# The expert layer of a graph and mixture-of-experts block: 35 pairs of blocks written out instead of 36, and a loop behind them that starts with an odd pair

## The chip, the cores and the metric

The kernel runs on one core of one Trainium2 chip. The metric is the time of one execution on the device, in microseconds (us), as the median of several runs. The engines are called PE (TensorE), DVE (VectorE), ACT (ScalarE), POOL (GpSimd) and SP (SyncE). All times below come from the three runs of the kernel before, or from one execution that the profiler recorded.

## What is computed

The input is 1250 nodes of width 512 and 40000 edges. A first part normalises the nodes, runs an attention over the edges and a linear attention beside it, and adds both. The part that matters here is the expert layer behind it:

```python
h = _ln(x, ln1_g, ln1_b).reshape(T, D)          # T = 1250, D = 512
logits = (h @ Wr) @ codebook.T / TEMP            # 64 experts
vals, idx = jax.lax.top_k(softmax(logits), 2)    # two experts a node, weights w
eh = silu(h @ W1[e] + b1[e])                     # 512 -> 256, for each expert e
eo = eh @ W2[e] + b2[e]                          # 256 -> 512
moe = sum of w * eo over the node's two experts
shared = (silu(h @ Ws1 + bs1) @ Ws2 + bs2) * 0.25   # 512 -> 1024 -> 512, every node
f = silu(_ln(moe + shared) @ Wf1 + bf1) @ Wf2 + bf2
return x + moe + shared + f
```

The 1250 nodes make 2500 assignments to 64 experts. With the reference's own inputs an expert gets from 7 to 88 of them: 59 experts have at most 64, five have more (71, 73, 79, 84 and 88).

## The kernel before

**Blocks and pairs.** The rows of an expert are cut into blocks of `R` = 64. Every expert has at least one block, so the inputs above fill 64 + 5 = 69 blocks. Blocks are numbered through, expert by expert, and two neighbouring blocks make a pair, which fills the 128 partitions. The number of blocks is only known on the chip. The kernel therefore has `PAIRS0` = 36 pairs (72 blocks) written out for every engine, and behind them a loop over two pairs at a time, which runs where there are more blocks. The bound of the loop, `H`, is worked out by DVE into `last`: (max(blocks, 69) - 1) >> 2, and every engine loads it. With `H` = 17 the loop is skipped and 2H + 2 = 36 pairs are done. A block without rows is worked on like any other; its lists of rows hold a number out of bounds, which the indirect DMAs leave out.

**One step of the expert loop.** Step p of PE has five parts, in this order:

- `hidden(p)` (L1739): the 512 to 256 product of pair p, with the weights `W1` of its two blocks,
- `result(p - 1)` (L1757): the 256 to 512 product of the pair before, with `W2`,
- the parts of `BESIDE[p]`: the shared network, cut into half products `("hidden", i, half)` (L1646) and thirds of a row tile `("shared", t, third)` (L1657, L1660), and a bias product (L1720); `parts_beside()` spreads these 50 parts over the `PAIRS0` steps in equal shares of columns,
- `hidden_transposes(p)` (L1747),
- `transposes(p + 2)` (L1729): the gathered rows `Zg` of the pair after next.

**Who feeds it.** POOL's queue has, for each p, the gather of pair p + 2 (L603) once `transposes(p)` is done, then the scatter of pair p - 1 (L608) once ACT has copied its result from PSUM (`eo`, L1347). So the gather that `transposes(p + 3)` needs at the end of step p + 1 stands behind the scatter of pair p - 1, and that behind `result(p - 1)` in step p. In steps 2 to 11 an addition on POOL (L624) stands between scatter and gather. SP loads the weights: for pair p, the two `W1` of 0.5 MB (L482) once `hidden(p - 2)` is done and the two `W2` (L485) once `result(p - 2)` is done. Buffers `Zg`, `hgT`, `eh`, `ehT` and `eo` are double, by the parity of the pair, and the weights lie in four places, two for each parity.

**The tail.** After the last result PE does the shared rows of tiles 8 and 9 (L1657, L1660), then the last network (L1802, L1810, L1818). POOL sends the last scatter, SP waits for both parities' scatters (`y_out[0]`, `y_out[1]`) and reads all of `y_d` back as `Yt` (L512). DVE weighs and adds the two results of each node (L1138), sums up the statistics, and works out the scale factors (L1147, L1149) from ACT's square roots (L1382); ACT normalises into `fz` (L1389), which PE transposes (L1802).

Of the kernel before, what the change touches and what calls it, by code (L numbers as in the profile page):

```python
# [6 lines left out]
F32 = mybir.dt.float32  # L7
# [25 lines left out]
PAIRS0 = 36  # L33
NP = 52
# [140 lines left out]
def block_kernel(nc, A, out):  # L175
    ctx = ExitStack()
    with ctx:
# [44 lines left out]
        carry = keep("carry", [1, 4, 1], F32)  # L222
# [183 lines left out]
        y_out = [sem(f"y_out{u}") for u in range(2)]  # L406
        yt_in = [sem(f"yt_in{i}") for i in range(YB)]
# [16 lines left out]
        def _(sp):  # L424
# [50 lines left out]
            def owners(g):  # L475
                return nc.values_load_multi_w_load_instructions(
                    owner[0:1, 4 * g:4 * g + 4] if isinstance(g, int) else owner[0:1, bass.ds(4 * g, 4)],
                    engines=[mybir.EngineType.SP], min_val=0, max_val=E - 1,
                    skip_runtime_bounds_check_because="an expert's number, held to E - 1 as it is made")[1]
# [7 lines left out]
            def group_weights(h):  # L487

                e = owners(h + 1)
                for u in range(2):  # L490
                    at_least(sp, h_done, 2 * h + u + 1)
                    first_weights(e[2 * u], 2 * u)
                    first_weights(e[2 * u + 1], 2 * u + 1)
                    at_least(sp, e_done, 2 * h + u + 1)
                    second_weights(e[2 * u], 2 * u)
                    second_weights(e[2 * u + 1], 2 * u + 1)

            for h in range(-1, PAIRS0 // 2 - 1):
                group_weights(h)
            H = sp.value_load(last[0:1, 0:1], min_val=PAIRS0 // 2 - 1, max_val=NP // 2 - 1)  # L500
# [22 lines left out]
        def _(gp):  # L523
# [68 lines left out]
            gp.drain().then_inc(idxg_made, PAIRS0 - 2)  # L592
            gp.drain().then_inc(idxs_made, PAIRS0 - 2)
# [31 lines left out]
            H = gp.value_load(last[0:1, 0:1], min_val=PAIRS0 // 2 - 1, max_val=NP // 2 - 1)  # L625
            with gp.If(H > PAIRS0 // 2 - 1):
                with gp.Fori(PAIRS0 // 2 - 1, H) as h:
                    for u in range(2):
                        wait_alone(tr_done, 2 * h + u + 3, 0)
                        nc.gpsimd.tensor_copy(idxg[:, u, :], gat[:, bass.ds(2 * h + u + 4, 1)]).then_inc(idxg_made, 1)  # L630
                        wait_alone(idxg_made, 2 * h + u + 1, 1)
                        gather(u, idxg[:, u, :])
                        wait_alone(e_read, 2 * h + u + 2, 2)
                        nc.gpsimd.tensor_copy(idxs[:, 1 - u, :], lst[:, bass.ds(2 * h + u + 1, 1)]).then_inc(idxs_made, 1)
                        wait_alone(idxs_made, 2 * h + u + 1, 3)
                        scatter(1 - u, idxs[:, 1 - u, :])
# [8 lines left out]
            for u in range(2):  # L645
                wait_alone(zg_in[u], 16 * H + 32, 0)
# [4 lines left out]
        def _(v):  # L651
# [377 lines left out]
            for k, M in ((0, M1), (1, M2)):  # L1029
# [4 lines left out]
                if k == 0:  # L1034
# [6 lines left out]
                    V_.tensor_scalar(last_i[:, :], counted[:, 0:1], -1.0, None, ALU.add)  # L1041
# [78 lines left out]
            H = v.value_load(last[0:1, 0:1], min_val=PAIRS0 // 2 - 1, max_val=NP // 2 - 1)  # L1120
            with v.If(H > PAIRS0 // 2 - 1):
                with v.Fori(PAIRS0 // 2 - 1, H) as h:
                    for u in range(2):
# [746 lines left out]
```

## Time and profile before

| | |
|---|---|
| three runs, median (lowest to highest) | 888.22 us (887.15 to 889.78) |
| the profiled execution's own time | 888.11 us |
| its span | 886.1 us, 11946 instructions |
| granted TensorE clock, mean | 0.996 of full speed |
| moved by DMA | 129.81 MB, mean 146 GB/s |

The span is the time from the first to the last instruction that the profiler saw. The execution's own time is 2.0 us longer, the start and end around the span. Rows of the timeline merge instructions of one line that follow each other; a matmul's length is modelled and reaches into the next row, so the time that a piece takes on PE is the difference between two starts. The expert loop's steps stand between about 546 and 817 us, the tail behind them.

### The profile page before, as it was taken

The numbers are of one execution on the slowest core, as the hardware profiler recorded it, in microseconds if no ns is written. First come the engines' busy times: TensorE is split into PE (matmuls) and PEld (weight loads), VectorE is DVE, ScalarE is ACT, GpSimd is POOL, SyncE is SP. The second block draws the span as 40 slices with busy tenths as digits, with TensorE's granted clock in tenths as the row PEclk, the third lists the DMA queues.
The fourth block names the chain that finished last, engine by engine and source line by source line (L and its number), as shares of the span: only waits on it lengthen the run. The fifth ranks groups of instructions, "written<-read, shape, count | busy, mean of one in ns | idle before, by whom it ended". The sixth has DMA issues, their size and how long they took to land.

```text
span 886.1 us, 11946 instructions
## 1 busy us (share of the span) xinstructions
PE 844.7 (95%) x3978; PEld 492.3 (56%) x3978; DVE 517.3 (58%) x1317; ACT 287.5 (32%) x560; POOL 153.1 (17%) x168
## 2 busy tenths in 40 slices
PE   3999999999989999999999999999999999999897
PEld 2565556655567444444456587456456545654464
DVE  7787677666776999999855584222223222222472
ACT  4531111200105666666334332223122212222283
POOL 6100002300100000000000211344422222222340
PEclk9999999999999999999999999999999999999999
DMA  9410000000327350510211524898898888895723
GB/s 274 166 49 1 1 1 1 1 0 1 136 96 173 84 117 1 116 49 1 68 62 46 181 106 163 276 314 317 302 320 318 321 315 289 320 317 209 201 54 94
DMA packets 41340, 129.81 MB, mean 146 GB/s; under 512 B 8393, under 2 KB 8835, under 8 KB 40639
## 3 DMA queue, kind: packets, MB, share of 16 engines
q1 hardware_dynamic: 32955, 110.76, 39.0%
q0 software_dynamic: 7872, 17.94, 5.6%
q8 instruction: 33, 0.54, 0.3%
q10 hardware_dynamic: 452, 0.34, 0.2%
q14 instruction: 28, 0.23, 0.1%
HBM read 118.48 MB, written 19.68 MB: 156 GB/s over the span
## 4 chain that ended last, share of the span: by engine, by line
PE 69%; DVE 12%; DMA 6%; issue 5%; DVEq 4%; ACT 2%; SPq 1%; POOL 1%; POOLq 0%; ACTq 0%
PE ps L1480 8%; DVE att L934 7%; PE ps L1739 7%; PE ps L1660 6%; PE ps L1757 6%; PE ps L1646 6%; DMA Zg<-z_d,gat 4%; PE ps L1458 4%; PE ps L1524 4%; PE ps L1611 4%; PE ps L1532 4%; PE ps L1441 3%; PE ps L1602 2%; PE ps L1575 2%; PE ps L1729 2%
## 5 line engine op out<-in xcount | busy, mean ns | idle before, releaser
L1085 DVE TENSOR_SCALAR hgT<-ps,cols 128x128 f32<-128x128 f32 x152 | 51.8, 403 | 152.1 <-PE ps L1729 142.1
L934 DVE TENSOR_TENSOR att<-es,C 125x832 f32<-125x832 f32 (+1 forms) x120 | 116.2, 1010 | 4.7 <-ACT es L1262 4.0
L1262 ACT ACTIVATE es<-ps 125x832 f32<-125x832 f32 (+1 forms) x120 | 95.4, 867 | 54.7 <-PE ps L1564 53.9
L1575 PE MATMUL ps<-att,V 125*64 125x416 f32 (+1 forms) x480 | 96.7, 525 | 5.5 <-DVE att L934 4.5
L1660 PE MATMUL ps<-Ws_s,hsT 128*125 128x512 f32 x160 | 75.0, 607 | 0.0
L1646 PE MATMUL ps<-hT,Ws_s 128*128 128x250 f32 x320 | 72.8, 379 | 0.4 <-issue 0.4
L1480 PE MATMUL ps<-mW,xnT 128*125 128x512 f32 x160 | 72.2, 594 | 0.0
L1739 PE MATMUL ps<-W,hgT 128*64 128x256 f32 x576 | 70.1, 385 | 0.4 <-DVE hgT L1085 0.4
L1646 PEld LDWEIGHTS ps<-hT,Ws_s 128*128 128x128 f32 x320 | 58.9, 189 | 19.4 <-issue 13.2
L1757 PE MATMUL ps<-W,ehT 128*64 128x512 f32 x288 | 68.0, 592 | 0.7 <-ACT ehT L1339 0.7
L608 POOL DMA_INDIRECT y_d<-eo,lst x35 | 35.6, 1018 | 177.2 <-ACT eo L1347 177.2
L753 DVE TENSOR_SCALAR ohB<-iotaW,key 125x200 bf16<-125x200 f16 x320 | 64.6, 265 | 0.0
L1575 PEld LDWEIGHTS ps<-att,V 125*64 125x64 f32 x480 | 29.1, 136 | 56.1 <-issue 31.5
L1564 PE MATMUL ps<-Qst,Kst 128*125 128x416 f32 (+1 forms) x240 | 56.9, 370 | 1.8 <-DVE C L895 0.7
L1347 ACT COPY eo<-ps 128x512 f32<-128x512 f32 x36 | 21.1, 585 | 114.7 <-PE ps L1757 114.7
L1339 ACT ACTIVATE ehT<-ps,b1T 128x64 f32<-128x64 f32 x144 | 33.4, 317 | 74.5 <-PE ps L1747 71.1
L1564 PEld LDWEIGHTS ps<-Qst,Kst 128*125 128x125 f32 x240 | 41.2, 185 | 28.8 <-ACT es L1262 18.4
L1660 PEld LDWEIGHTS ps<-Ws_s,hsT 128*125 128x125 f32 x160 | 28.1, 187 | 46.0 <-issue 46.0
L1739 PEld LDWEIGHTS ps<-W,hgT 128*64 128x64 f32 x576 | 38.1, 136 | 20.4 <-DVE hgT L1085 0.5
L566 POOL DMA_DIRECT2D z_d<-yz x10 | 5.4, 536 | 239.2 <-DVE yz L969 239.2
L1441 PEld LDWEIGHTS ps<-ohB,ohA 125*128 125x128 bf16 x320 | 30.8, 114 | 28.2 <-issue 25.5
L757 DVE TENSOR_TENSOR Cx<-Cx,ps 128x200 f32 x80 | 28.5, 356 | 29.9 <-PE ps L1441 17.2
(249 smaller groups left out, 1204.1 us busy)
## 6 DMA issues: line engine op xcount, KB each, us to landing
W<-in_W SPq DMA_DIRECT2D x144, 512.0 KB
Kst<-qk_d SPq DMA_DIRECT2D x32, 156.2 KB, 5.6
Qst<-qk_d SPq DMA_DIRECT2D x32, 156.2 KB, 5.8
Yt<-y_d SPq DMA_DIRECT2D x10, 448.0 KB
Ws_s<-in_Ws SPq DMA_DIRECT2D x2, 2048.0 KB, 9.9
qk_d<-qk_hi POOLq DMA_DIRECT2D x4, 625.0 KB, 3.6
qk_d<-qk_lo POOLq DMA_DIRECT2D x4, 625.0 KB, 4.7
z_d<-yz POOLq DMA_DIRECT2D x10, 250.0 KB, 2.7
```

The lines of the kernel that those rows point to most:

```text
L753: i = V_.tensor_scalar(ohB[:, s, j, :], iotaW[:, :], key[:, bass.ds(k + j, 1)], None, ALU.is_equal)
L934: V_.tensor_tensor(att[:, n % AB, :, 0:w], es[:, n % EB, :, 0:w], C[:, s, o:o + w].unsqueeze(1).to_broadcast([P, 2, w]), ALU.mult).then_in ...
L1085: i = V_.tensor_scalar(hgT[:, u, k, :], bank(u, 128, 128, k * 128), col("g1", k), col("b1ln", k), ALU.mult, ALU.add)
L1262: S_.activation(es[:, n % EB, :, 0:w], scores_of(n, w), ACT.Exp, scale=float(DK) ** -0.5).then_inc(s_exp, 1)
L1441: i = MM(bank(b, WN), ohA[:, s, :, j], ohB[:, s, j, :], start=j == 0, stop=j == EG - 1)
L1480: i = MM(bank(b, D, P), xnT[:, k, t * P:t * P + P], mW[:, 1 + w, k, :], start=k == 0, stop=k == KD - 1)
L1564: k = MM(scores_of(n, w)[:, j, :], Kst[:, h % 4, s * P:s * P + P], Qst[:, h % 4, o:o + w], start=True, stop=True)
L1575: k = MM(sums_of(i, 64 * j, 64, w), V[:, s, pair, j:j + 2, :], att[:, n % AB, j, 0:w], start=s == 0, stop=s == T - 1, skip_group_check=True)
L1646: j = MM(bank(b, 250, 128, 250 * half), Ws1_s[:, k, (2 * g + half) * 128:(2 * g + half + 1) * 128], hT[:, k, c * 250:c * 250 + 250], start ...
L1660: i = MM(bank(b, D, P), hsT[:, t // 2 % 2, k, (t % 2) * P:(t % 2) * P + P], Ws2_s[:, k, :], start=False, stop=k == DSH // 128 - 1)
L1739: i = MM(bank(2, DFF, 128, DFF * u)[R * j:R * j + R], hgT[:, u, k, R * j:R * j + R], W1[2 * u + j][:, k, :], start=k == 0, stop=k == KD - ...
L1757: i = MM(bank(4 + u, D)[R * j:R * j + R], ehT[:, u, m, R * j:R * j + R], W2[2 * u + j][:, m, :], start=m == 0, stop=m == 1, skip_group_che ...
```

## The change

`PAIRS0` becomes 35. The written-out part then ends with an even pair (34, buffers of parity 0), where it ended with an odd one (35, parity 1). The loop behind it still does two pairs an iteration, now first the odd and then the even one, and its bound becomes (max(blocks, 67) - 3) >> 2, with 2H + 3 pairs done. With 69 blocks H is 16, the lower bound, the loop is skipped, and 35 pairs (70 blocks) are done. The closing scatter is that of parity 0. SP's wait at the end for both parities is replaced: POOL waits for `y_out[1]` after it has sent the last scatter, does an addition of one element and raises `odd_written`; SP waits for `odd_written` and then for `y_out[0]`. The queue of SP is written per pair instead of per two pairs, in the same order. `parts_beside()` is unchanged but spreads over 35 steps.

```diff
-PAIRS0 = 36
+PAIRS0 = 35
...
-        carry = keep("carry", [1, 4, 1], F32)
+        carry = keep("carry", [1, 5, 1], F32)
...
+            def pair_weights(p, u, e):
+
+                at_least(sp, h_done, p - 1)
+                first_weights(e[0], 2 * u)
+                first_weights(e[1], 2 * u + 1)
+                at_least(sp, e_done, p - 1)
+                second_weights(e[0], 2 * u)
+                second_weights(e[1], 2 * u + 1)
+
+            for p in range(0, PAIRS0, 2):
+                e = owners(2 * p)
+                pair_weights(p, 0, e[0:2])
+                if p + 1 < PAIRS0:
+                    pair_weights(p + 1, 1, e[2:4])
+            H = sp.value_load(last[0:1, 0:1], min_val=PAIRS0 // 2 - 1, max_val=NP // 2 - 2)
...
-            for u in range(2):
-                sp.wait_ge(y_out[u], 16 * H + 16)
+            sp.wait_ge(odd_written, 1)
+            sp.wait_ge(y_out[0], 16 * H + 32)
...
-            gp.drain().then_inc(idxg_made, PAIRS0 - 2)
-            gp.drain().then_inc(idxs_made, PAIRS0 - 2)
+            gp.drain().then_inc(idxg_made, PAIRS0 - 1)
+            gp.drain().then_inc(idxs_made, PAIRS0 - 1)
...
-            wait_alone(y_out[1], 16 * H, 2)
-            nc.gpsimd.tensor_copy(idxs[:, 1, :], lst[:, bass.ds(2 * H + 1, 1)]).then_inc(idxs_made, 1)
-            wait_alone(idxs_made, 2 * H + 1, 3)
-            wait_alone(e_read, 2 * H + 2, 1)
-            scatter(1, idxs[:, 1, :])
+            wait_alone(y_out[0], 16 * H + 16, 2)
+            nc.gpsimd.tensor_copy(idxs[:, 0, :], lst[:, bass.ds(2 * H + 2, 1)]).then_inc(idxs_made, 1)
+            wait_alone(idxs_made, 2 * H + 3, 3)
+            wait_alone(e_read, 2 * H + 3, 1)
+            scatter(0, idxs[:, 0, :])
+            wait_alone(y_out[1], 16 * H + 16, 4).then_inc(odd_written, 1)
...
-                    V_.tensor_scalar(last_i[:, :], counted[:, 0:1], -1.0, None, ALU.add)
+                    V_.tensor_scalar(last_i[:, :], counted[:, 0:1], -3.0, None, ALU.add)
...
             with pe.If(H > PAIRS0 // 2 - 1):
                 with pe.Fori(PAIRS0 // 2 - 1, H) as h:
...
                     hidden(2 * h + 3, h + 1, 1)
                     result(2 * h + 2, h + 1, 0)
                     hidden_transposes(2 * h + 3, 1)
                     transposes(2 * h + 5, h + 2, 1)
-            result(2 * H + 1, H, 1)
+                    hidden(2 * h + 4, h + 2, 0)
+                    result(2 * h + 3, h + 1, 1)
+                    hidden_transposes(2 * h + 4, 0)
+                    transposes(2 * h + 6, h + 3, 0)
+            result(2 * H + 2, H + 1, 0)
...
-            pe.wait_ge(tr_read, 2 * H + 4)
-            pe.wait_ge(h_read, 2 * H + 2)
-            pe.wait_ge(x_read, 2 * H + 2)
-            pe.wait_ge(e_read, 2 * H + 2)
+            pe.wait_ge(tr_read, 2 * H + 5)
+            pe.wait_ge(h_read, 2 * H + 3)
+            pe.wait_ge(x_read, 2 * H + 3)
+            pe.wait_ge(e_read, 2 * H + 3)
```

The other hunks change the bounds of `value_load` and the order of the pairs in the loops of POOL, DVE and ACT in the same way. Lines from about L407 on stand 1 to 6 lines lower in the changed kernel.

**Where the instructions move.** The spreading over 35 steps moves parts between neighbouring steps. On PE the ends of steps 5, 6 and 7 read before (L1646 is a half product of the shared network as x4, two as x8, L1747 and L1729 close a step, and the rows left out are the pair's own products):

```order
L1646 MATMUL ps<-hT,Ws_s 128x250 x8
L1747 MATMUL ps<-ident,eh 128x128 x2
L1729 MATMUL ps<-ident,Zg 128x128 x4
...
L1646 MATMUL ps<-hT,Ws_s 128x250 x4
L1747 MATMUL ps<-ident,eh 128x128 x2
L1729 MATMUL ps<-ident,Zg 128x128 x4
...
L1646 MATMUL ps<-hT,Ws_s 128x250 x8
L1747 MATMUL ps<-ident,eh 128x128 x2
L1729 MATMUL ps<-ident,Zg 128x128 x4
```

and in the changed kernel, where the same three lines are L1652, L1753 and L1735:

```order
L1652 MATMUL ps<-hT,Ws_s 128x250 x8
L1753 MATMUL ps<-ident,eh 128x128 x2
L1735 MATMUL ps<-ident,Zg 128x128 x4
...
L1652 MATMUL ps<-hT,Ws_s 128x250 x8
L1753 MATMUL ps<-ident,eh 128x128 x2
L1735 MATMUL ps<-ident,Zg 128x128 x4
...
L1652 MATMUL ps<-hT,Ws_s 128x250 x4
L1753 MATMUL ps<-ident,eh 128x128 x2
L1735 MATMUL ps<-ident,Zg 128x128 x4
```

The two steps with one and two half products have changed places: the step with only one is now step 7, behind two full ones.

POOL's queue, from the end of the loop to the first addition of the tail, reads before (the last rows of the loop are left out; L600 is the one-element addition that a wait stands before, L638 the copy of the list of rows, L608 the scatter, L644 the addition of the tail):

```order
L599 REGISTER_ALU
L600 TENSOR_TENSOR carry<-eps 1x1
L638 ISA
L638 COPY idxs<-lst 128x1
L600 TENSOR_TENSOR carry<-eps 1x1
L599 REGISTER_ALU
L600 TENSOR_TENSOR carry<-eps 1x1
L608 DMA y_d<-eo,idxs 2500x512
L644 TENSOR_TENSOR XR<-XR,HM 125x512 x10
```

and in the changed kernel:

```order
L604 ISA
L605 TENSOR_TENSOR carry<-eps 1x1
L643 ISA
L643 COPY idxs<-lst 128x1
L604 REGISTER_ALU
L605 TENSOR_TENSOR carry<-eps 1x1 x2
L613 DMA y_d<-eo,idxs 2500x512
L605 TENSOR_TENSOR carry<-eps 1x1
L650 TENSOR_TENSOR XR<-XR,HM 125x512 x10
```

One addition of one element, the one that raises `odd_written`, now stands between the last scatter and the ten additions of the tail.

## Rows read from the trace of the kernel before

**Rows 1.** The page, part 1: busy microseconds, share of the span, instructions
```profile
PE 844.7 (95%) x3978; PEld 492.3 (56%) x3978; DVE 517.3 (58%) x1317; ACT 287.5 (32%) x560; POOL 153.1 (17%) x168
```

**Rows 2.** Stretches: length, busy PE, PEld, DVE, ACT, POOL, clock, DMA share, GB/s
```profile
546.00:812.00 266.00, 262.01 (x1396) 148.69 (x1394) 69.01 (x188) 61.39 (x198) 82.75 (x79) 1.00 0.87 306
```

**Rows 3.** What PE waited for, 540 to 836 us: total, times, longest
```profile
PE ps L1729 <- DMA Zg<-z_d,gat: 4.0, 6, 1.0
```

**Rows 4.** Timeline of PE: start, length, [idle before]; one step, one half product
```profile
593.60 1.96 PE L1646 MATMUL ps<-hT,Ws_s 128*128 128x250 f32 x8
595.39 0.39 PE L1747 MATMUL ps<-ident,eh 128*128 128x128 f32 x2
...
802.76 1.95 PE L1739 MATMUL ps<-W,hgT 128*64 128x256 f32 x16
804.53 1.89 PE L1757 MATMUL ps<-W,ehT 128*64 128x512 f32 x8
806.35 2.84 PE L1660 MATMUL ps<-Ws_s,hsT 128*125 128x512 f32 x6
809.03 0.39 PE L1747 MATMUL ps<-ident,eh 128*128 128x128 f32 x2
809.26 0.65 PE L1729 MATMUL ps<-ident,Zg 128*128 128x128 f32 x4
809.83 1.95 PE L1739 MATMUL ps<-W,hgT 128*64 128x256 f32 x16
```

**Rows 5.** Timeline of PE: two of the six stalls in the expert loop
```profile
658.21 0.75 PE L1729 MATMUL ps<-ident,Zg 128*128 128x128 f32 x4 [0.97 <-DMA Zg<-z_d,gat]
...
757.33 0.75 PE L1729 MATMUL ps<-ident,Zg 128*128 128x128 f32 x4 [0.48 <-DMA Zg<-z_d,gat]
```

**Rows 6.** Timeline of POOL: the gathers that these two waited for, and a later one
```profile
649.92 1.03 POOL L603 DMA_INDIRECT Zg<-z_d,gat  x1 [0.30 <-issue]
...
749.61 1.03 POOL L603 DMA_INDIRECT Zg<-z_d,gat  x1 [0.30 <-issue]
...
809.18 1.03 POOL L603 DMA_INDIRECT Zg<-z_d,gat  x1 [0.30 <-issue]
```

**Rows 7.** Tail, timelines of PE, ACT and DVE: shared rows to scale factors
```profile
817.70 1.94 PE L1757 MATMUL ps<-W,ehT 128*64 128x512 f32 x8 [0.73 <-ACT ehT L1339]
...
835.70 0.63 PE L1802 MATMUL ps<-ident,fz 125*128 125x125 f32 x4
...
836.84 0.30 ACT L1382 ACTIVATE rs<-mv,eps 125x1 f32<-125x1 f32 x1
...
828.33 1.59 DVE L1138 SCALAR_TENSOR_TENSOR HM<-Yt,wtop,HM 125x512 f32<-125x512 f32 x2 [9.95 <-DMA Yt<-y_d]
...
837.17 0.16 DVE L1147 RECIPROCAL rs<-rs 125x1 f32<-125x1 f32 x1 [1.07 <-ACT rs L1382]
```

**Rows 8.** Tail, timelines of POOL and SP: the last scatter, the first read-back
```profile
814.93 1.01 POOL L608 DMA_INDIRECT y_d<-eo,lst  x1 [4.72 <-ACT eo L1347]
...
821.17 1.02 POOL L608 DMA_INDIRECT y_d<-eo,idxs  x1 [0.56 <-issue]
...
823.93 10.37 SPq L512 DMA_DIRECT2D Yt<-y_d  x20
```

**Rows 9.** Half-microsecond stretches after the last two scatters, columns as rows 2
```profile
816.50:817.00 0.50, 0.48 (x4) 0.28 (x3) 0.50 (x1) 0.47 (x3) 0.04 (x1) 1.00 0.31 99
...
822.50:823.00 0.50, 0.50 (x3) 0.26 (x2) 0.00 (x0) 0.00 (x0) 0.00 (x0) 1.00 0.08 1
```

**Rows 10.** DMA by queue, 814 to 830 us: packets, MB, share
```profile
q0 software_dynamic: 160, 0.05, 1.2%
```

**Rows 11.** The page, part 6: a plain write to HBM from POOL, us to landing
```profile
z_d<-yz POOLq DMA_DIRECT2D x10, 250.0 KB, 2.7
```

**Rows 12.** Timelines of POOL and PE: a gather on idle DMA engines
```profile
540.12 1.03 POOL L603 DMA_INDIRECT Zg<-z_d,gat  x1 [0.30 <-issue]
...
543.52 0.75 PE L1729 MATMUL ps<-ident,Zg 128*128 128x128 f32 x4 [0.36 <-DMA Zg<-z_d,gat]
```

More of the change, by code:

```diff
@@ L406, in block_kernel @@
         y_out = [sem(f"y_out{u}") for u in range(2)]
+        odd_written = sem("odd_written")
         yt_in = [sem(f"yt_in{i}") for i in range(YB)]
@@ L485, in second_weights @@
                 sp.dma_start(W2[s][:, :, :], A["W2"][bass.ds(e, 1)].rearrange("e (p m) n -> p (e m) n", m=2)).then_inc(w2_in[s], 16)
-            def group_weights(h):
-                e = owners(h + 1)
-                for u in range(2):
[L491 to L500, printed above, removed]
+            def pair_weights(p, u, e):
[11 more added lines that the diff above has]
+            H = sp.value_load(last[0:1, 0:1], min_val=PAIRS0 // 2 - 1, max_val=NP // 2 - 2)
             with sp.If(H > PAIRS0 // 2 - 1):
                 with sp.Fori(PAIRS0 // 2 - 1, H) as h:
-                    group_weights(h)
-            for u in range(2):
-                sp.wait_ge(y_out[u], 16 * H + 16)
+                    e = owners(4 * h + 6)
+                    pair_weights(2 * h + 3, 1, e[0:2])
+                    pair_weights(2 * h + 4, 0, e[2:4])
+            sp.wait_ge(odd_written, 1)
+            sp.wait_ge(y_out[0], 16 * H + 32)
             y_v = y_d.rearrange("(t p k) d -> t p k d", p=P, k=TOPK)
@@ L1119, in _ @@
                 rows_turned(p + 2, p % 2)
-            H = v.value_load(last[0:1, 0:1], min_val=PAIRS0 // 2 - 1, max_val=NP // 2 - 1)
+            H = v.value_load(last[0:1, 0:1], min_val=PAIRS0 // 2 - 1, max_val=NP // 2 - 2)
             with v.If(H > PAIRS0 // 2 - 1):
                 with v.Fori(PAIRS0 // 2 - 1, H) as h:
-                    for u in range(2):
-                        hidden_kept(2 * h + u + 2, u)
-                        rows_turned(2 * h + u + 4, u)
+                    for i in range(2):
+                        hidden_kept(2 * h + i + 3, 1 - i)
+                        rows_turned(2 * h + i + 5, 1 - i)
             def output(t):
@@ L1775, in _ @@
                 transposes(p + 2, p // 2 + 1, p % 2)
-            H = pe.value_load(last[0:1, 0:1], min_val=PAIRS0 // 2 - 1, max_val=NP // 2 - 1)
+            H = pe.value_load(last[0:1, 0:1], min_val=PAIRS0 // 2 - 1, max_val=NP // 2 - 2)
             with pe.If(H > PAIRS0 // 2 - 1):
                 with pe.Fori(PAIRS0 // 2 - 1, H) as h:
-                    hidden(2 * h + 2, h + 1, 0)
-                    result(2 * h + 1, h, 1)
-                    hidden_transposes(2 * h + 2, 0)
-                    transposes(2 * h + 4, h + 2, 0)
                     hidden(2 * h + 3, h + 1, 1)
```

36 lines of the change are left out of this document (18 added, 18 removed).

## The prediction

> **What bounds the kernel now.** I read the page's busy line first: PE is busy for 844.7 us of a span of 886.1, DVE for 517.3, ACT for 287.5, POOL for 153.1 [rows 1]. A step taken off PE's queue is therefore a step off the span, unless PE waits in that stretch for somebody else. The stretch of the expert loop, 546 to 812 us, says how much it does: PE is busy for 262.01 of 266.00 us, at a granted clock of 1.00 of full speed, 2.4 GHz. The DMA engines are close behind, with a share of 0.87 at 306 GB/s [rows 2]. The waits of PE name the whole difference: 4.0 us in six waits, the longest 1.0, all of them for the gather of `Zg` [rows 3]. So PE sets the pace of the loop, and transfers take 4.0 us of it. In the tail PE, ACT and DVE hand work to each other; that is looked at below.
>
> **Does the change do what it says?** The pair that goes must be one without rows. The counts in the section on what is computed give 64 + 5 = 69 blocks, so 35 pairs hold them all with one block spare. The trace agrees. After the scatter of pair 34, issued at 814.93 [rows 8], 0.5 us at 99 GB/s moved 50 KB, which is 24 rows of 2 KB; after that of pair 35, issued at 821.17, the stretch in which its data would move shows 1 GB/s [rows 9]. All that the software queue moved from 814 to 830 us is 0.05 MB [rows 10]. Pair 35 is empty, H becomes (69 - 3) >> 2 = 16, and the loop behind is skipped as now.
>
> **The change part by part.**
>
> *The pair's own work on PE.* By differences of starts [rows 4]: hidden 804.53 - 802.76 = 1.77, result 806.35 - 804.53 = 1.82, the two hidden transposes 809.26 - 809.03 = 0.23, the four row transposes 809.83 - 809.26 = 0.57. Together 4.39 us, with nothing beside it: PE has no gap between these rows. The shared parts stay, in number and length; they only sit in 35 steps. The end of the loop keeps its form too: the last step before it and the last result do the same work on the other parity. Term: **-4.4 us**.
>
> *The pair's work elsewhere.* Four weight loads of 0.5 MB, a gather, a scatter without rows, four scalings on DVE and one copy, one copy and four activations on ACT. None of these engines is behind which PE waited in the loop [rows 3]. Term: 0. If that cover were gone it could only be a gain, since all of it is work removed.
>
> *The waits for the gathers.* A gather is sent after the result of step p, and needed at the end of step p + 1. The result before the late gather ended at 806.35, the gather was issued at 809.18, 2.83 us later [rows 4, 6]. From there to its transposes PE has the shared parts b(p), 0.23 + 0.57 + 1.77 + 1.82 + 0.23 = 4.62 us of pair work, and b(p + 1). So the gather has b(p) + b(p + 1) + 1.8 us. A third of a shared row tile is 809.03 - 806.35 = 2.68 us, a half product 595.39 - 593.60 = 1.79 [rows 4]; two thirds in a row give 7.2 us, one half product beside two give 1.79 + 3.58 + 1.8 = 7.2 too. Measured from issue to the stalled transposes, gathers took 658.21 - 649.92 = 8.29 and 757.33 - 749.61 = 7.72 us [rows 5, 6], and the stalls of 0.97 and 0.48 are what is over, to 0.2 us. Short neighbours make stalls, but not always, since a stall or a long step lets the transfers catch up. I went through both tables of parts and counted the neighbours with b(p) + b(p + 1) up to 5.6 us, from step 1 on, without the last three, behind which the weights run out: 18 before and 15 after. In six places something was late before. Some move: the one at the end of step 6 goes to step 7 (the order rows above), where the single half product now stands. The same share of 15 gives 4.0 x 15 / 18 = 3.3 us, a gain of 0.7; nothing but the backlog decides where, so 0 is as near. I take the middle, **-0.3 us**. The bounds: -4.0 if all six vanish, and +2.0 if two of the neighbours that got by now stall by the longest wait of 1.0 each.
>
> *The tail.* It starts from the last result, so all of it moves forward with it. Two things are new there. First, the last scatter now carries the 24 rows of pair 34, where it was empty. The empty one took 823.93 - 821.17 = 2.76 us from issue to SP's first read-back [rows 8]; a plain write of 250 KB from POOL lands after 2.7 us [rows 11], a gather of up to 128 rows on idle engines is used 543.52 - 540.12 = 3.40 us after its issue [rows 12]. So the rows cost from -0.1 to +0.6 us; I take 0.2, nearer the write. Second, the read-back has some slack: DVE, after its first tiles, waits 1.07 us at 837.17 for ACT's square root of 836.84, and ACT is late because it copies what PE transposed at 835.70, when the shared rows were done [rows 7]. A read-back up to 1.07 us later changes nothing. Term: **0**; without that cover, +0.2.
>
> *The new handshake.* POOL's extra wait is for a scatter sent one step earlier, 6.2 us before [rows 8], and queued behind it on POOL are only the additions of the tail, which wait for DVE. `odd_written` rises about one issue (1.02 us) after the last scatter starts, while that one needs 2.76 to land. SP has nothing else to do. Term: 0.
>
> By the Trainium skill, page "DMA: Bandwidth & Descriptors", section "Anatomy of one DMA", a DMA has a fixed cost of about 2 us, most of it the receipt of the write, and the receipt is slowest when the target is HBM. If an empty scatter had no receipt to wait for, the real one would cost up to 2 us more, an estimate from that page, and 0.9 of it would be beyond the slack. The trace speaks against: the empty scatter's 2.76 us already are a full write's 2.7.
>
> **Sum.** 888.11 - 4.4 - 0.3 = 883.4 us for the profiled execution. It stands 0.1 under the median of the three runs, 888.22, so I predict **883.5 us**.
>
> **The rivals.**
>
> *Transfers pace the loop.* For it: a share of 0.87 and 306 GB/s. A pair's weights are 4 x 0.5 MB = 2.1 MB, at 306 GB/s 6.9 us, which would be saved instead of 4.4: 881.3 us. At the extreme all waits go: 883.5 + 0.3 - 4.0 = 879.8. Against: PE lost only 4.0 us in all, and the pair removed is the last one, behind which nothing else is loaded. Chance 0.07.
>
> *The gain is partly given back.* The new grouping stalls more, up to +2.0, or the last scatter with its rows is beyond the slack, 3.4 - 2.76 would not be enough, so it would have to land like a gather in the loaded loop: 8.29 - 2.76 - 1.07 = +4.5 at the very most, in a tail where no weights are moving. With one of them in part, 884.7 to 886.5 us. The rule on the write receipt belongs here: a scatter that moves rows lands later than an empty one, here by 1.07 + 0.9 us at most if it is to cost the 0.9, and that gives 883.5 + 0.9 = 884.4; chance of it 0.06, inside the forecast's own range. The rest of this rival has 0.12.
>
> *The loop is entered.* If more than 70 blocks were counted, 35 pairs would be followed by an iteration of two. This is the one that ends slower. Its steps have no shared parts to hide behind: transfers then set the pace, at least the 6.9 us of weights a pair, at most the 2.83 + 8.29 us from a result to the next rows. That is 883.5 + 2 x 6.9 = 897 to 883.5 + 2 x 11.1 = 906 us. It decides from block 71 on. Against: 69 blocks, and no rows moved in pair 35 [rows 9, 10]. Chance 0.02.
>
> **The numbers.** About 0.3%, 2.7 us, is what a measurement of this kernel can tell from no change, so faster means under 885.5. The forecast, 882.3 to 884.7, has 0.78 with the receipt in it, transfers that pace 0.07, given back 0.12, the loop 0.02, and 0.01 is left for what I do not see. Faster: 0.78 + 0.07 + half of 0.12 = 0.91, of which I take one point off for the spread of the runs, 887.15 to 889.78: 0.90. Within 0.3%: 0.07. Slower: 0.03. The range that leaves out no more than 2 in 10 reaches half way into the two neighbours: 881.7 to 885.3.
>
> **What would show it.** In the profile after: 35 copies to `eo`, 140 weight loads, 37 gathers, and PE busy for about 840.3 us. The start of the first product of the loop is the same as now, and the last result starts 4 to 5 us before 817.70. PE's waits for `Zg` sum to 2.5 to 4.5 us, with one at step 7 rather than at step 6. SP's read-back starts 2.7 to 3.4 us after the last scatter, and DVE's wait for ACT's square root shrinks from 1.07 by what the scatter gained; if that wait is gone the tail's term was wrong. If PE's waits changed by more than 1 us, the term of the gathers was. Copies into `idxg` on POOL, or more than 35 pairs, would make all of it wrong.

## The result and the profile after

| | before | changed |
|---|---|---|
| median of 9 runs | 887.92 us (885.59 to 890.45) | 883.93 us (881.92 to 885.45) |
| ratio, 95% interval | | 0.9949 [0.9936, 0.9961] |
| profiled execution, time and span | 888.11 and 886.1 us | 884.23 and 882.5 us |
| first `hidden` starts | 544.62 us | 546.57 us |
| loop: from there to the last `result` | 273.08 us | 267.88 us |
| tail: from there to the end of the span | 68.40 us | 68.05 us |

The changed kernel is faster by 0.51%, 4.5 us (3.5 to 5.7), by the ratio; the two medians differ by 4.0 us. The two profiles differ by 3.6 us in span. That difference is made of three parts: 546.57 - 544.62 = +1.95 us ahead of the loop, -5.20 us in it, -0.35 us behind it. The lines of the page for the changed kernel (L1745 is `hidden`, L1763 `result`, L1735 the row transposes):

```profile
span 882.5 us, 11853 instructions
...
PE 841.4 (95%) x3948; PEld 490.4 (56%) x3948; DVE 515.1 (58%) x1312; ACT 286.3 (32%) x555; POOL 151.9 (17%) x167
...
W<-in_W SPq DMA_DIRECT2D x140, 512.0 KB, 6.7
```

The counts are those forecast: 140 loads of `W` for 144, 37 gathers and 35 copies to `eo`. PE is busy 3.3 us less than the 844.7 of [rows 1]. Its waits from 535 to 836 us, which answer to [rows 3] (total, times, longest):

```profile
PE ps L1735 <- DMA Zg<-z_d,gat: 2.7, 4, 1.0
...
PE ps L1745 <- DVE hgT L1091: 1.0, 1, 1.0
PE ps L1763 <- ACT ehT L1345: 0.9, 1, 0.9
```

The waits for `Zg` are 2.7 us in four places, for 4.0 us in six. PE's timeline, with the first product of the loop, the four stalls, and the last result:

```profile
546.57 1.95 PE L1745 MATMUL ps<-W,hgT 128*64 128x256 f32 x16 [0.98 <-DVE hgT L1091]
...
591.50 0.75 PE L1735 MATMUL ps<-ident,Zg 128*128 128x128 f32 x4 [0.50 <-DMA Zg<-z_d,gat]
...
697.89 0.75 PE L1735 MATMUL ps<-ident,Zg 128*128 128x128 f32 x4 [0.74 <-DMA Zg<-z_d,gat]
...
758.93 0.75 PE L1735 MATMUL ps<-ident,Zg 128*128 128x128 f32 x4 [0.46 <-DMA Zg<-z_d,gat]
...
791.35 0.75 PE L1735 MATMUL ps<-ident,Zg 128*128 128x128 f32 x4 [0.97 <-DMA Zg<-z_d,gat]
...
814.45 1.94 PE L1763 MATMUL ps<-W,ehT 128*64 128x512 f32 x8 [0.94 <-ACT ehT L1345]
```

The stalls stand at the ends of steps 5, 19, 27 and 31. The tail, in the timelines of POOL, SP, ACT and DVE, which answers to [rows 7, 8]:

```profile
817.91 1.03 POOL L613 DMA_INDIRECT y_d<-eo,idxs  x1 [0.57 <-issue]
818.97 0.18 POOL L605 TENSOR_TENSOR carry<-eps 1x1 f32<-1x1 f32 x1
...
820.25 10.31 SPq L517 DMA_DIRECT2D Yt<-y_d  x20
...
833.58 0.30 ACT L1388 ACTIVATE rs<-mv,eps 125x1 f32<-125x1 f32 x1
...
833.91 0.16 DVE L1153 RECIPROCAL rs<-rs 125x1 f32<-125x1 f32 x1 [1.56 <-ACT rs L1388]
```

The addition at 818.97 raises `odd_written`, long before SP's read-back at 820.25. From the last scatter to the read-back it takes 820.25 - 817.91 = 2.34 us, for 2.76 before, although this scatter carries rows. DVE then waits 1.56 us for ACT's square root, for 1.07 before: the read-back came earlier, and what ended the wait is still ACT, behind PE's shared rows.

Further on in the tail PE waits 2.18 us for `fz` in both kernels, and the product behind it does not take equally long. In the kernel before (L1810) and in the changed one (L1816):

```profile
839.92 5.21 PE L1810 MATMUL ps<-fT,Wf_s 128*128 128x250 f32 x16 [0.67 <-ACT fT L1367]
...
836.67 3.65 PE L1816 MATMUL ps<-fT,Wf_s 128*128 128x250 f32 x16 [0.67 <-ACT fT L1373]
```

To the next start it is 844.97 - 839.92 = 5.05 us before, where the granted clock fell to 0.64 between 841 and 844 us, and 840.20 - 836.67 = 3.53 us after, where it stayed at 1.00. The time did not change: the product with `f1T` that follows starts 6.55 us after these rows in both (846.47 and 843.22), since in the changed kernel PE waits 1.56 us for ACT there, for 0.39 before.

**The 1.95 us ahead of the loop are not the change's.** No instruction moves there. Stretches of the profile (length, busy PE, PEld, DVE, ACT, POOL, granted clock, DMA share, GB/s) of the changed kernel:

```profile
513.00:519.00 6.00, 5.73 (x72) 5.41 (x72) 3.72 (x14) 1.32 (x3) 0.76 (x1) 0.86 0.01 3
519.00:522.00 3.00, 3.00 (x9) 2.34 (x9) 2.78 (x6) 0.00 (x0) 0.00 (x0) 0.50 0.00 0
522.00:525.00 3.00, 3.00 (x11) 2.51 (x10) 2.44 (x9) 0.00 (x0) 0.00 (x0) 0.65 0.26 59
525.00:528.00 3.00, 3.00 (x16) 2.69 (x15) 2.92 (x3) 1.53 (x3) 0.00 (x0) 1.00 1.03 370
```

and of the kernel before:

```profile
513.00:519.00 6.00, 4.94 (x71) 4.25 (x69) 3.85 (x13) 1.53 (x3) 0.76 (x1) 1.00 0.01 3
519.00:522.00 3.00, 3.00 (x18) 2.68 (x17) 2.66 (x4) 0.00 (x0) 0.00 (x0) 1.00 0.00 0
```

In the changed kernel's profile the granted clock is 0.50 of full speed from 519 to 522 us, which is 1.2 GHz, and 0.65 in the three after. Before it fell PE did the many small products that count the experts' rows. The 64 matmuls of the shared network behind them show the cost. In the changed kernel they start at 519.26 and the next line at 535.24:

```profile
519.26 16.14 PE L1652 MATMUL ps<-hT,Ws_s 128*128 128x250 f32 x64
535.24 1.54 PE L1707 MATMUL ps<-slots,rowhot 125*128 125x156 bf16 x20
```

15.98 us. In the kernel before:

```profile
519.70 13.76 PE L1646 MATMUL ps<-hT,Ws_s 128*128 128x250 f32 x64
533.30 1.54 PE L1701 MATMUL ps<-slots,rowhot 125*128 125x156 bf16 x20
```

13.60 us, the same work: 2.38 us less, and the rest of the 1.95 is a start that was 0.44 us later before. I looked at the stretch from 505 to 528 us in all 14 profiles of this study: the clock was lowered somewhere in it in 10 of them, in kernels with 36 pairs and with 35, and not in 4; the kernel before is one of the 4 and the changed one of the 10. `table_alone` and `table_again` below are one and the same kernel, profiled twice, the first time without the lowering and the second time with it. In 9 of the 10 the clock fell behind the small products, and the 64 matmuls took 14.8 to 16.5 us for 13.6; in `plain_waits` it fell ahead of them, at 504 to 510 us. The first `hidden` starts at 543.2 to 545.0 us in the four and at 544.3 to 547.6 in the others. Over many executions the two kernels are alike in this: the mean granted clock is 0.9942 over the nine of the changed kernel, and 0.9945 over 27 of the kernel before that were timed beside `table_alone`.

### The profile page after: what moved, and what is told of

The parts are those of the page before. It is cut to its first block, busy times and chain, and to the rows that moved or that the text cites. A ratio compares the mean times of both kernels' runs of the same rounds, so it can differ in the third digit from the quotient of the medians.

```text
span 882.5 us, 11853 instructions
## 1 busy us (share of the span) xinstructions
PE 841.4 (95%) x3948; PEld 490.4 (56%) x3948; DVE 515.1 (58%) x1312; ACT 286.3 (32%) x555; POOL 151.9 (17%) x167
## 4 chain that ended last, share of the span: by engine, by line
PE 68%; DVE 12%; DMA 6%; issue 5%; DVEq 4%; ACT 2%; POOL 1%; SPq 1%; POOLq 0%; ACTq 0%
PE ps L1486 8%; DVE att L940 7%; PE ps L1666 6%; PE ps L1745 6%; PE ps L1652 6%; PE ps L1763 6%; DMA Zg<-z_d,gat 5%; PE ps L1464 4%; PE ps L1530 4%; PE ps L1617 4%; PE ps L1538 4%; PE ps L1447 3%; PE ps L1608 2%; PE ps L1581 2%; PE ps L1735 2%
## 5 line engine op out<-in xcount | busy, mean ns | idle before, releaser
L1652 PE MATMUL ps<-hT,Ws_s 128*128 128x250 f32 x320 | 74.7, 388 | 0.4 <-issue 0.4
L1652 PEld LDWEIGHTS ps<-hT,Ws_s 128*128 128x128 f32 x320 | 60.7, 194 | 18.9 <-issue 12.1
L1745 PE MATMUL ps<-W,hgT 128*64 128x256 f32 x560 | 68.2, 385 | 1.0 <-DVE hgT L1091 1.0
L1763 PE MATMUL ps<-W,ehT 128*64 128x512 f32 x280 | 66.1, 592 | 0.9 <-ACT ehT L1345 0.9
L1745 PEld LDWEIGHTS ps<-W,hgT 128*64 128x64 f32 x560 | 37.1, 136 | 20.4 <-DVE hgT L1091 1.2
```

The costliest lines, as they stand in the source:

```text
L1652: j = MM(bank(b, 250, 128, 250 * half), Ws1_s[:, k, (2 * g + half) * 128:(2 * g + half + 1) * 128], hT[:, k, c * 250:c * 250 + 250], start ...
L1745: i = MM(bank(2, DFF, 128, DFF * u)[R * j:R * j + R], hgT[:, u, k, R * j:R * j + R], W1[2 * u + j][:, k, :], start=k == 0, stop=k == KD - ...
L1763: i = MM(bank(4 + u, D)[R * j:R * j + R], ehT[:, u, m, R * j:R * j + R], W2[2 * u + j][:, m, :], start=m == 0, stop=m == 1, skip_group_che ...
```

## The experiments

The prediction left three things to be shown. My theory: the gain is the pair's 4.4 us of work on PE, which sets the pace; the waits for `Zg` move a little, and come from the gather's place in POOL's queue; transfers are not the bound. The rivals: the regrouping of the shared parts brings the time, or the pair is worth the 6.9 us of its transfers. In the table, the loop and the waits for `Zg` (those over 0.2 us, in the loop) are from each profile; the ratio is to the kernel before, timed on the same chip.

| kernel | pairs | ratio, 95% interval | loop, us | waits for Zg, at the ends of steps |
|---|---|---|---|---|
| before | 36 | 1 | 273.08 | 4.0: 4, 6, 14, 17, 23, 27 |
| changed | 35 | 0.9949 [0.9936, 0.9961] | 267.88 | 2.7: 5, 19, 27, 31 |
| table_alone | 36 | 1.0002 [0.9986, 1.0017] | 276.28 | 4.1: 11, 14, 19, 27, 31 |
| table_again | 36 | one execution | 271.89 | 2.4: 12, 19, 31, 34 |
| pair_alone | 35 | 0.9961 [0.9946, 0.9975] | 267.84 | 2.7: 4, 14, 17 |
| loads_kept | 35 | 0.9949 [0.9934, 0.9964] | 268.44 | 2.9: 2, 12, 19, 27, 31 |
| loads_removed | 36 | 0.9997 [0.9983, 1.0012] | 273.03 | 3.1: 2, 6, 9, 14, 23 |
| plain_waits | 35 | 0.9941 [0.9928, 0.9954] | 269.19 | 3.6: 2, 4, 8, 14, 19, 24, 31 |
| constants_36 | 36 | one execution | 273.14 | 2.4: 14, 24, 27, 29 |
| gather_first_36 | 36 | 0.9953 [0.9936, 0.9969] | 269.31 | none |
| gather_first | 35 | 0.9901 [0.9886, 0.9915] | 264.19 | none |
| first_weights_first | 35 | 0.9892 [0.9864, 0.9920] | 262.76 | none |
| loop_entered | 33 + 2 | 0.9945 [0.9924, 0.9966] | 268.41 | 3.3: 14, 22, 33 |
| loop_taken_37 | 35 + 2 | 1.0097 [1.0071, 1.0124] | 282.26 | 5.2: 2, 19, 31, 35 |

### The table alone, and the pair alone

```diff
 # table_alone, on the kernel before
-        table[min(PAIRS0 - 1, done * PAIRS0 // total)].append(part)
+        table[min(PAIRS0 - 2, done * (PAIRS0 - 1) // total)].append(part)
 # pair_alone, on the changed kernel
-        table[min(PAIRS0 - 1, done * PAIRS0 // total)].append(part)
+        table[min(PAIRS0 - 1, done * (PAIRS0 + 1) // total)].append(part)
```

> The kernel before with its 36 pairs, but with the shared parts spread over the first 35 steps as in the changed kernel, so that step 35 has only the pair's own work. Theory (the gain is the pair's own 4.4 us on PE, and the regrouping moves only the waits for gathers): between -1.3 and +0.3 us against before in the loop, plus what the bare step 35 exposes, since its hidden transposes, activation and result now follow each other with nothing beside them: about +1 us for the copy of the hidden rows. Together within 1 us of before, and PE's waits for Zg sum to 2.5 to 4.5 us. Rival (the regrouping is what brings the time): 2 us or more faster than before. Rival (transfers pace): no change.

> The changed kernel with 35 pairs, but with the shared parts spread as over 36 steps, the parts of step 35 joined to step 34. Theory: -4.4 us from the removed pair, and the stalls of before in steps 4 to 27 at their old places, so 3.4 to 4.6 us faster than before and within 1 us of the changed kernel; PE's waits for Zg sum to 3.5 to 4.5 us, with those of before at the ends of steps 4, 6, 14, 17, 23 and 27. Rival (the regrouping is a good part of the gain): only 2 to 3 us faster than before. Rival (transfers pace the loop): 6 us or more.

The table alone changed nothing (-0.1 to +0.2%). The pair alone gave 0.9961, 3.5 us of 888.5 (2.2 to 4.8), against 4.5 with both; the intervals overlap, so whether the table adds a microsecond can't be told. Its loop, 267.84 us, is that of the changed kernel to 0.04. The rival of the regrouping falls. Of my expectation for the places, three of six came true (4, 14, 17).

The first profile of `table_alone` had a loop of 276.28 us, 3.2 over the kernel before, which its times don't show. Step 20 was long. PE's timeline there:

```profile
698.26 0.75 PE L1729 MATMUL ps<-ident,Zg 128*128 128x128 f32 x4 [1.78 <-DMA Zg<-z_d,gat]
698.94 2.96 PE L1739 MATMUL ps<-W,hgT 128*64 128x256 f32 x16
701.68 2.62 PE L1757 MATMUL ps<-W,ehT 128*64 128x512 f32 x8
```

and the stretches around it (columns as above):

```profile
700.00:702.00 2.00, 2.00 (x12) 1.19 (x10) 0.48 (x3) 0.00 (x0) 0.00 (x0) 0.50 0.99 385
702.00:704.00 2.00, 2.00 (x8) 0.39 (x4) 0.37 (x1) 0.00 (x0) 0.00 (x0) 0.72 0.54 212
```

After a wait of 1.78 us the granted clock fell to 0.50, and `hidden` took 2.74 us and `result` 2.55 to the next start, for 1.77 and 1.82. So a stall can cost nearly its length again. The same kernel was profiled once more:

> The kernel before with 36 pairs and the shared parts spread over the first 35 steps, once more, for its profile: in the first one step 20 took 1.7 us longer than the same step of the changed kernel, with its products slower at an unchanged number. Theory (a granted clock that fell for one moment after a wait of 1.8 us): a chance event that does not return here; the loop from the first hidden product to the last result takes 273 to 275 us. Rival (the regrouping with 36 pairs is slower): 276 us again, with the same step long.

Its loop was 271.89 us, with no wait over 0.9 us and no long step: chance, as the theory said, and even below the 273 I had given. A wait of 1.55 us in `pair_alone` and one of 1.51 in `loop_entered` were followed by a clock of 1.00, so the length alone does not decide. The tail shows it better: the wait of 2.18 us for `fz` is there in all 14 profiles, and the clock fell behind it in 12, but not in the changed kernel and in `loads_kept`.

### The weight loads alone

```diff
 # loads_kept, on the changed kernel
+            pair_weights(PAIRS0, 1, e[2:4])
...
+            for j in (2, 3):
+                sp.wait_ge(w1_in[j], 16 * (PAIRS0 // 2 + 1))
+                sp.wait_ge(w2_in[j], 16 * (PAIRS0 // 2 + 1))
             sp.wait_ge(odd_written, 1)
 # loads_removed, on the kernel before
-                for u in range(2):
+                for u in range(1 if isinstance(h, int) and h == PAIRS0 // 2 - 2 else 2):
                     at_least(sp, h_done, 2 * h + u + 1)
```

In `loads_removed` PE's waits for the weights of pair 35 ask for one load less.

> The changed kernel, to which the four weight loads of a pair 35 are given back (2.1 MB that nobody reads, sent where the kernel before sends them), without its products, gather or scatter. Theory (PE paces the loop): within 0.5 us of the changed kernel, so 3.6 to 4.9 us faster than before. Rival (transfers pace, and a pair is worth its 6.9 us of weights): most of the gain is gone, within 1.5 us of before.

> The kernel before with its 36 pairs, but without the four weight loads of pair 35, whose products then read what lies in their places; pair 35 has no rows, so no output depends on it. Theory (PE paces the loop): within 0.5 us of before, and PE's waits for Zg unchanged to 1 us, since the loads fall in the last three steps. Rival (transfers pace): 2 us or more faster than before.

With the four loads given back the ratio is 0.9949, the changed kernel's own; with them taken away from the kernel before it is 0.9997. The last pair's 2.1 MB are worth nothing that shows in either; the intervals reach some 1.3 us to each side. The rival of the transfers falls for this pair, by both runs.

### Gathers ahead of scatters

```diff
             gather(1, gat[:, 1:2])
+            gp.wait_ge(tr_done, 1)
+            gather(0, gat[:, 2:3])
             for p in range(PAIRS0):
-                gp.wait_ge(tr_done, p + 1)
-                gather(p % 2, gat[:, p + 2:p + 3])
+                gp.wait_ge(tr_done, p + 2)
+                gather((p + 1) % 2, gat[:, p + 3:p + 4])
                 if p:
                     gp.wait_ge(e_read, p)
                     scatter((p - 1) % 2, lst[:, p - 1:p])
```

The loop behind has the same shift.

> The changed kernel with POOL's queue in another order: the gather of pair p + 3 is sent before the scatter of pair p - 1, once the transposes of pair p + 1 are done, and no longer behind the result of pair p - 1. It is then issued about 5 us earlier in its step. Theory (the waits for Zg come from the gather's place behind the scatter): PE's waits for Zg, 2.7 us in the changed kernel, fall under 0.3 us, and the time is 2 to 3.5 us below the changed kernel, near 881.3 us, 6.5 to 8 us below the kernel before. Rival (the DMA engines are full, and what is late then is the weights): PE waits for the transfers of W instead, and the time is within 1 us of the changed kernel.

> The kernel before, 36 pairs, with the same new order on POOL. Theory: its 4.0 us of waits for Zg go, 3 to 4.5 us faster than before, and the difference to the same edit with 35 pairs is the removed pair's own work alone, 4.4 us in the loop. Rival (the pair is worth its transfers, 6.9 us): that difference is 6 us or more.

881.18 us and 0.9901, 8.8 us below the kernel before, a little more than the 6.5 to 8 expected. On the same chip `plain_waits`, which does what the changed kernel does, had 883.90 and 0.9941, so the new order is worth 2.7 us by the medians and 3.6 by the ratios, and 267.88 - 264.19 = 3.7 in the loop of the profiles (5.0 against the profile of `plain_waits`, which had more waits). What PE waits for from 540 to 836 us (L1747 is `hidden`, L1765 `result`):

```profile
PE ps L1747 <- DMA W<-in_W: 1.1, 3, 0.7
PE ps L1747 <- DVE hgT L1093: 1.0, 1, 1.0
PE ps L1765 <- ACT ehT L1347: 0.8, 1, 0.8
```

No wait for `Zg` is left, as the theory said; 1.1 us of waits for `W` have come up, as the rival said, but they are less than what went. With 36 pairs the same edit gives 0.9953. The difference of the two is 0.52%, 4.6 us, the removed pair with the gathers' waits out of the way in both: the 4.4 us of PE's work, not 6.9, which lies just outside what the two intervals leave together, some 2.6 to 6.6 us. In the profiles the loops differ by 269.31 - 264.19 = 5.1 us, 0.6 of it waits for `W`, 1.7 us with 36 pairs and 1.1 with 35.

### First weights first

```diff
 # SP's order, on gather_first:   W1(p), W2(p), W1(p + 1), W2(p + 1), ...
 # becomes:                       W1(p + 1), W2(p), W1(p + 2), W2(p + 1), ...
+                first_of(p, e[0:2])
+                if old is not None:
+                    second_of(p - 1, old)
...
+                    first_of(p + 1, e[2:4])
+                    old = e[2:4]
+                second_of(p, e[0:2])
```

> The changed kernel with gathers ahead of scatters, and in SP's queue the W1 of pair p + 1 ahead of the W2 of pair p. In the profile with gathers ahead PE waited 1.1 us for transfers of W, each time at the first product of a step. Theory (W1 is needed 1.8 us before the W2 that stands ahead of it in the queue): those waits go and no wait for W2 comes up, 1 us or less faster than with gathers ahead alone, near 880.3 us. Rival (the transfers only change places, and W2 or the gathers are late by the same): no gain, or a loss of up to 1 us.

878.94 us, ratio 0.9892, 9.6 us below the kernel before. It is 0.8 us below `gather_first` by the ratios, with intervals that overlap, so the times do not show a gain of this step by itself; the profile does, 262.76 us of loop for 264.19. All that PE waits for from 540 to 836 us (L1762 is `hidden`, L1780 `result`, L1825 and L1833 are in the tail):

```profile
PE ps L1825 <- ACT fz L1412: 2.2, 1, 2.2
PE ps L1762 <- DVE hgT L1108: 1.0, 1, 1.0
PE ps L1780 <- ACT ehT L1362: 0.8, 1, 0.8
PE ps L1833 <- ACT fT L1390: 0.7, 1, 0.7
```

Not one wait for a transfer is listed. PE is busy for 261.92 of the loop's 262.76 us, and the one wait in it is that of 0.84 for its last product; the wait of 0.98 stands ahead of the first. This version beats both kernels.

### The loop, priced

```diff
 # loop_entered, on the changed kernel
-PAIRS0 = 35
+PAIRS0 = 33
 # loop_taken_37, on the changed kernel
-                    V_.tensor_scalar(counted[:, 0:1], base_s[0:1, E:E + 1], 1.0 / R, 2.0 * PAIRS0 - 3.0, ALU.mult, ALU.max)
+                    V_.tensor_scalar(counted[:, 0:1], base_s[0:1, E:E + 1], 1.0 / R, 2.0 * PAIRS0 + 1.0, ALU.mult, ALU.max)
```

> The changed kernel with 33 pairs written out, so that with 69 blocks the loop behind runs once and does pairs 33 and 34: again 35 pairs in all. The shared parts are spread over 33 steps. This measures what the loop would have cost. Theory (bare steps are paced by the gathers and weights): the two looped steps take 2 x 6.9 to 2 x 11.1 us where two written-out ones without their shared parts take 2 x 4.4, so 5 to 13 us slower than the changed kernel. Rival (the loop costs no more than its branches): within 2 us of it.

> The changed kernel with the lower bound of counted blocks raised from 67 to 71, so that its loop runs once although 69 blocks are filled, and 37 pairs are done, 35 and 36 without rows. This is the rival that ends slower, by itself. Its price as predicted: 13.8 to 22 us over the changed kernel, 897 to 906 us. Corrected theory, from the run with 33 pairs written out, whose two looped steps took 6.3 and 5.5 us and not 6.9 or more, because the weights that they wait for were loaded beside longer steps: 11 to 13 us over the changed kernel, 895 to 897 us. And if a scatter without rows takes longer than one with 24 rows, SP's first read-back is again 2.7 us or more after the last scatter, since pair 36 has no rows; if the parity or the handshake decided, 2.3 to 2.4 us.

With two of the 35 pairs in the loop, the ratio is 0.9945, no slower than with all written out. I had expected 5 to 13 us. The two looped steps on PE:

```profile
801.59 1.95 PE L1745 MATMUL ps<-W,hgT 128*64 128x256 f32 x16 [0.40 <-DMA W<-in_W]
803.34 1.92 PE L1763 MATMUL ps<-W,ehT 128*64 128x512 f32 x8
...
807.21 0.75 PE L1735 MATMUL ps<-ident,Zg 128*128 128x128 f32 x4 [1.51 <-DMA Zg<-z_d,idxg]
807.89 1.95 PE L1745 MATMUL ps<-W,hgT 128*64 128x256 f32 x16
...
813.40 1.94 PE L1763 MATMUL ps<-W,ehT 128*64 128x512 f32 x8 [0.58 <-ACT ehT L1345]
```

From 801.59 to 813.40 us, 11.8 us for both: 2 x 4.4 of work, waits of 1.51 and 0.58, the last of which the changed kernel has too (0.94), and 0.9 us in gaps too short to be listed; a wait of 0.40 stands ahead. So the bare steps cost 3 us more at most. The step that failed in my price is that a bare step is paced by the 6.9 us of its weights: PE waited 0.40 us for weights in these two. That they had been loaded beside the longer steps ahead is my reading. In the profile's loop 0.5 us of it is left, 268.41 for 267.88; waits for `Zg` ahead were shorter by 0.9 and the last wait by 0.4, and the remaining 1 us I did not follow up.

With two pairs more than the changed kernel, the loop costs 1.0097 - 0.9949 = 1.48%, 13.1 us (10 to 17 by the intervals), and 282.26 - 267.88 = 14.4 us in the profile. It lies between the rival's price of 13.8 to 22 us and my corrected 11 to 13, and its interval reaches into both; the profile is with the former. Where they went:

```profile
821.70 0.98 PE L1735 MATMUL ps<-ident,Zg 128*128 128x128 f32 x4 [2.99 <-DMA Zg<-z_d,idxg]
822.61 3.33 PE L1745 MATMUL ps<-W,hgT 128*64 128x256 f32 x16
```

Two bare pairs are 8.8 us. A wait of 2.99 us for rows stands between them, then `hidden` takes 3.16 us to the next start at 825.77, for the 1.77 of [rows 4], with the granted clock at 0.84 and 0.88 in the two stretches around it. That is 13.2 of the 14.4 us; the rest I did not follow up.

```profile
818.00:824.00 6.00, 3.01 (x16) 1.71 (x16) 1.28 (x4) 1.46 (x5) 3.06 (x8) 0.84 0.77 282
824.00:830.00 6.00, 5.07 (x30) 2.52 (x28) 1.88 (x6) 1.45 (x5) 0.99 (x4) 0.88 0.00 0
```

POOL and SP:

```profile
812.63 1.02 POOL L613 DMA_INDIRECT y_d<-eo,lst  x1 [4.77 <-ACT eo L1353]
...
814.76 1.05 POOL L608 DMA_INDIRECT Zg<-z_d,idxg  x1 [0.53 <-issue]
...
832.96 1.02 POOL L613 DMA_INDIRECT y_d<-eo,idxs  x1 [0.55 <-issue]
...
835.13 4.94 SPq L517 DMA_DIRECT2D Yt<-y_d  x11
```

The rows that PE waited for until 821.70 are those of the gather of 814.76, sent behind the scatter of 812.63: 821.70 - 814.76 = 6.9 us, with no shared parts to cover them. So it was the rows that held up the bare pairs, not their weights.

### Plain waits, and the closing scatter

```diff
 # plain_waits, on the changed kernel
-            sp.wait_ge(odd_written, 1)
-            sp.wait_ge(y_out[0], 16 * H + 32)
+            sp.wait_ge(y_out[1], 16 * (PAIRS0 // 2))
+            sp.wait_ge(y_out[0], 16 * (PAIRS0 // 2 + 1))
...
-            wait_alone(y_out[1], 16 * H + 16, 4).then_inc(odd_written, 1)
 # constants_36, on the kernel before
-                sp.wait_ge(y_out[u], 16 * H + 16)
+                sp.wait_ge(y_out[u], 16 * (PAIRS0 // 2))
```

> The changed kernel without the handshake: POOL's extra wait and its addition are gone, and SP waits for both y_out itself, against constants that hold for 35 pairs. Theory: no change in time, within 0.5 us of the changed kernel, and SP's first read-back again 2.3 to 2.4 us after the last scatter, which then shows that the 2.76 us of the kernel before belong to its scatter without rows. Rival (the double wait on SP is what takes longer): read-back 2.7 us or more after the scatter here too.

> The kernel before, 36 pairs, whose SP waits for the two y_out at the end against the constant 288 instead of a value worked out from H, in the same order. It looks at the time from the last scatter to SP's first read-back, which was 2.71 to 3.23 us in five profiles with 36 pairs, 2.34 to 2.43 in six with 35, and 2.17 in the one with 37, whose last scatter is without rows too. Theory (the form of SP's wait, a value of a register for both semaphores, takes the 0.4 us): 2.3 to 2.4 us. Rival (it is the closing scatter of parity 1): 2.7 us or more. No change in time is expected from either, since the read-back has slack.

The handshake costs nothing: 0.9941 without it, 0.9949 with it. From the last scatter to the read-back the six profiles with 36 pairs have 2.71 to 3.23 us, the seven with 35 have 2.34 to 2.43, `plain_waits` at the upper end. I took it for the missing rows. Then `loop_taken_37`, whose last scatter is without rows too, had 835.13 - 832.96 = 2.17 us (above), and that theory fell. Then I took it for the form of SP's wait, and with constants it was no shorter:

```profile
822.37 1.02 POOL L608 DMA_INDIRECT y_d<-eo,idxs  x1 [0.56 <-issue]
...
825.58 10.23 SPq L512 DMA_DIRECT2D Yt<-y_d  x20
```

3.21 us. What still fits all profiles is that 36 pairs close with the place of parity 1 and the others with that of parity 0; no run tried it by itself, so the cause stays open. The time does not depend on it, since DVE waited for ACT in the tail in either case.

## Why the prediction was right

883.5 us were predicted, 883.93 measured, inside the range; faster, as forecast.

- **The pair's own work, -4.4 us.** Right. The pair of kernels without waits for `Zg` differs by 4.6 us, and the kernels with the pair's work and without it by 3.5 (`pair_alone`) and 4.5 (the change). In the profiles the loop is shorter by 5.20: 4.4 of work and 1.3 of waits for `Zg`, less 0.2 by which the wait before the last `result` grew, and less 0.3 of which 0.2 is idle time too short to be listed.
- **The pair's work elsewhere, 0.** Right for the loads, which were tried in both directions. The indirect DMAs and the work of ACT and DVE were not tried by themselves.
- **The waits for the gathers, -0.3 us, between -4.0 and +2.0.** The profiles say 4.0 before and 2.7 after, -1.3, inside the bounds, but more than the 1 us by which the prediction itself called the term wrong. But kernels with the same loop as before had 3.1 and 2.4, and with the same loop as the changed one 2.9 and 3.6, so the size and the sign of this term are not settled, and it is small. The step that failed is the count of neighbours in both tables as a forecast of places: I said that the stall at the end of step 6 goes to step 7, and in no profile was there one; they were at 5, 19, 27 and 31. Of these, 19 and 31 are the table's: they are there in all six profiles that spread over 35 steps and send the gathers last, and in none that spread over 36. 14 is there in all four that spread over 36, but also in `table_alone`, `plain_waits` and `loop_entered`. The others come and go with the execution. The cause, the gather's place behind the scatter, was right: moved ahead, all of it went. The busy transfers are part of it, since the stalled gathers took 5.9 to 10.2 us in these profiles, for 3.4 with the engines idle [rows 12].

One term was missing as well. The sum gave each gather b(p) + b(p + 1) + 1.8 us, from a delay of 2.83 us behind the result. In steps 2 to 11 POOL's addition stands in between, and the delay is longer. In step 4 of the changed kernel:

```profile
579.85 2.84 PE L1666 MATMUL ps<-Ws_s,hsT 128*125 128x512 f32 x6
...
582.37 1.31 POOL L629 TENSOR_TENSOR XR<-XR,rows 125x512 f32<-125x512 f32 x1
583.84 1.04 POOL L608 DMA_INDIRECT Zg<-z_d,gat  x1 [0.16 <-issue]
```

583.84 - 579.85 = 3.99 us. So the gather for the end of step 5 had 1.2 us less than the sum gives it, and it came late although b(4) + b(5), a third and two half products, is 6.3 us and not among the fifteen short neighbours.
- **The tail, 0.** Right in the sum: 68.40 us before, 68.05 after. Wrong in the size inside it: I gave the last scatter +0.2 us for its rows, between -0.1 and +0.6, and the time to the read-back fell by 0.42. DVE's wait for the square root, which was to shrink from 1.07 us, grew to 1.56. The Trainium skill (page "DMA: Bandwidth & Descriptors", section "Anatomy of one DMA") puts most of a fixed cost of about 2 us on the receipt of the write. My estimate from it, that a real write could cost up to 2 us more than an empty one, is not borne out: 2.34 us with 24 rows, 2.17 to 3.23 without any.
- **The handshake, 0.** Right: 0.9941 without it.
- **The first product starts as now.** Wrong by 1.95 us, and I had not thought of a clock that falls in one execution and not in the next. In the comparison of the two profiles it hid more than a third of the loop's gain; the last `result` starts 3.25 us earlier, and not 4 to 5. It is also in PE's busy time, 841.4 us for the forecast 840.3: ahead of the loop PE was busy 2.1 us longer than before, in the tail, where the clock had fallen before and not after, 1.2 us shorter.
- **The rivals.** Transfers that pace the loop: they fall for the last pair. The loop, at 13.8 to 22 us, measured 13.1 (10 to 17), but its lower end came from 6.9 us of weights a pair, and what PE waited for was one late gather, so the nearness of the number is luck. The range's upper end has a slip: half way into the neighbour up to 886.5 is 885.6 and not 885.3; the result lies under both.

## What to carry to other kernels

A unit of work taken off the engine that sets the pace is worth its own length there, by differences of starts, and the share of the DMA engines, 0.87 here, does not say that its transfers are worth anything: those of this loop's last pair were worth nothing that showed. When a slow queue carries both what the next steps need and what the last one leaves, look at their order first: here it was worth 2.7 to 3.7 us, nearly as much as the removed pair, for a few lines. And compare two profiles stretch by stretch from a common mark before explaining their difference, with the granted clock beside it.

## What the runs showed that I had not expected

- The granted TensorE clock falls to 0.50 between 505 and 528 us in some executions and not in others (10 of 14 profiles, 9 of them behind the small products), and the 64 matmuls there then take up to 2.9 us more than 13.6 (16.46 in `first_weights_first`).
- A wait of PE for 1.78 us was followed by some 3 us at a lowered clock and cost 1.7 us more; one of 2.99 us likewise, at 1.4 us; waits of 1.51 and 1.55 us were not. One of 2.18 us in the tail was in 12 of 14 profiles, and in the pair of before and changed it cost nothing, because PE then waited for ACT.
- Some late gathers are there in every profile of a table (19 and 31, or 14), the rest are not the same from one execution to the next.
- Closing with 36 pairs, whose last scatter is empty, the read-back starts 2.71 to 3.23 us after it; with 35 pairs and 24 rows 2.34 to 2.43; with 37 pairs and an empty one again 2.17: open.
